# A two-convolution block on one core: one semaphore for each quarter of the parts, two kinds of transfers issued by ScalarE instead of SyncE, and the bias matmuls of a step in one block

## What is computed

```python
x = x + _L0_conv_ref(_gn(x), L0_conv_weight, L0_conv_scale)
x = x + _L1_conv_ref(_gn(x), ...)
# _L1_conv_ref: r = relu(bn(w_r x + b)); ker = w_s r + b_s
for ki in range(K):
    for kj in range(K):
        out = out + xp[:, :, :, ki:ki + H, kj:kj + W] * ker[:, :, ki * K + kj][:, :, None]
```

## Time and profile before

| | before |
|---|---|
| median of 3 runs | 2220.75 us (2215.48 to 2227.02) |
| profiled execution | 2222.71 us, span 2220.9 us |
| TensorE / VectorE / ScalarE / GpSimd busy | 78% / 61% / 48% / 46% |
| mean granted TensorE clock | 0.896 of full |
| DMA queues q1 (SyncE) and q10 (ScalarE), share of 16 engines | 77.3% and 3.5% |

### The profile page before, as it was taken

How to read it: one execution, slowest core, us unless ns; L and a number is a source line. 1 busy time by engine, 2 the same in 40 slices (tenths; PEclk the granted TensorE clock), 3 DMA queues, 4 the chain that set the end, 5 groups by cost and what they waited for, 6 DMA issues and landing times.

```text
span 2220.9 us, 39147 instructions
## 1 busy us (share of the span) xinstructions
PE 1724.5 (78%) x15168; PEld 737.5 (33%) x15168; DVE 1358.6 (61%) x1652; ACT 1061.5 (48%) x758; POOL 1020.8 (46%) x905
## 2 busy tenths in 40 slices
PE   3497878868798686877868788686986869878885
PEld 2242333323333232333323333232332323323332
DVE  5374756747477574765747567564764747657564
ACT  1354455535455453554534555454554535545453
POOL 2154444445355443554534444443553435544563
PEclk8798988989899897998989899898997989979897
DMA  4768888788888888888788798887888888887894
GB/s 96 181 179 198 205 200 217 194 194 206 195 206 220 196 201 190 204 210 204 203 197 198 191 214 210 193 215 181 205 217 189 191 191 207 208 195 196 198 250 117
DMA packets 224281, 436.46 MB, mean 197 GB/s; under 512 B 89214, under 2 KB 136751, under 8 KB 219951
## 3 DMA queue, kind: packets, MB, share of 16 engines
q1 hardware_dynamic: 207968, 408.27, 77.3%
q10 hardware_dynamic: 16128, 25.70, 3.5%
HBM read 336.06 MB, written 84.93 MB: 190 GB/s over the span
## 4 chain that ended last, share of the span: by engine, by line
issue 32%; POOL 29%; SPq 13%; DMA 10%; PE 7%; DVE 5%; ACT 3%; POOLq 0%; ACTq 0%; DVEq 0%
POOL folded L383 29%; DMA parts_dram<-parts 7%; SPq L318 6%; PE ybank L581 3%; SPq L288 3%; DVE prod L817 2%; SPq L258 2%; SPq L272 1%; DMA sums_dram<-osb 1%; DMA relu<-blocks 1%; PE ybank L523 1%; PE ybank L613 1%; ACT patches L449 1%; ACT blocks L459 1%; PE obank L592 1%
## 5 line engine op out<-in xcount | busy, mean ns | idle before, releaser
L383 POOL TENSOR_TENSOR folded<-prod 128x448 f32<-128x448 f32 x896 | 1009.1, 1140 | 1178.7 <-DVE prod L817 1178.5
L817 DVE TENSOR_TENSOR prod<-ybank,relu 128x896 f32<-128x896 f32 x896 | 960.8, 1090 | 379.9 <-PE ybank L581 312.7
L449 ACT ACTIVATE patches<-patches 64x1792 f16<-64x1792 f16 x448 | 745.4, 1708 | 514.0 <-DMA patches<-parts_dram 380.2
L581 PE MATMUL ybank<-patches,wspan 128*64 128x448 f16 x7168 | 863.6, 376 | 155.1 <-DVE prod L817 114.8
L581 PEld LDWEIGHTS ybank<-patches,wspan 128*64 128x64 f16 x7168 | 368.2, 114 | 674.3 <-issue 265.1
L592 PE MATMUL obank<-patches,wbias 128*32 128x448 f16 x3584 | 237.6, 390 | 118.5 <-ACT osb L437 118.5
L599 PE MATMUL obank<-folded,esum 128*32 128x448 f32 x1792 | 228.4, 583 | 1.5 <-POOL folded L383 1.5
L523 PE MATMUL ybank<-sgn,convw 128*128 128x448 bf16 x1008 | 205.1, 357 | 8.0 <-DVE prod L817 4.5
L613 PE MATMUL ybank<-back,blocks 128*128 128x128 f32 (+1 forms) x448 | 70.6, 310 | 168.7 <-ACT blocks L459 168.7
L829 DVE TENSOR_TENSOR xs<-ybank,xs 128x1024 f32<-128x1024 f32 (+1 forms) x64 | 61.9, 967 | 204.7 <-PE ybank L613 204.6
L592 PEld LDWEIGHTS obank<-patches,wbias 128*32 128x32 f16 x3584 | 79.2, 101 | 256.1 <-ACT osb L437 136.4
(11 more groups left out here) (92 smaller groups left out, 423.4 us busy)
## 6 DMA issues: line engine op xcount, KB each, us to landing
patches<-parts_dram SPq DMA_DIRECT2D x1232, 224.0 KB, 6.4
parts_dram<-parts SPq DMA_DIRECT2D x128, 256.0 KB, 2.8
xs<-x_dram SPq DMA_DIRECT2D x128, 196.0 KB, 5.0
sums_dram<-osb ACTq DMA_DIRECT2D x112, 224.0 KB, 5.7
rows<-sums_dram SPq DMA_DIRECT2D x112, 224.0 KB, 3.2
out_dram<-xs SPq DMA_DIRECT2D x128, 196.0 KB, 3.6
relu<-blocks SPq DMA_DIRECT2D x256, 49.0 KB
patches<-gb_dram SPq DMA_DIRECT2D x1, 784.0 KB
```

Source lines behind the costliest of these rows:

```text
L383: pool.tensor_tensor(folded[:, u % 8, :], prod[:, u % 2, 0, :], prod[:, u % 2, 1, :], ALU.add).then_inc(fold_done, 1)
L449: act.activation(X2[0:COPIED_ROWS, e % 2, at], X1[0:COPIED_ROWS, e % 3, at], ACT.Copy).then_inc(copied, 1)
L581: mm = pe.matmul(bank("unit", p, n)[64 * t:64 * t + 64, h, 0:N], wspan[0:STACK_ROWS[stack], stack, g, h, :], of_group(e, stack, g), start= ...
L817: dve.tensor_tensor(prod[:, u % 2].rearrange("m h (n c) -> m h n c", c=GC), bank("unit", p, n)[:, :, 0:N].rearrange("m h (n c) -> m h n c" ...
```

## The change

There are three edits.

1. `d_written` becomes four semaphores, one for each quarter. `parts_out(p, k)` now waits only until quarter k of the pair before has landed, `first_stack` waits for all four, and `high` for the quarter two before, whose buffer it writes again.
2. `rows` and `spread` are issued from ScalarE's queue. `spread(p + 1)` stands right after the second relu (unit 38), `spread(0)` before the first copies; `rows(e - 1)` stands at unit 7 of each step (`ROWS_AT`), behind the copies at units 4 and 5 and ahead of `sign` at unit 7 of the pair.
3. Both stacks of `bias(e)` are issued at unit 6 of the step; before, one was at unit 5 and one at unit 6.

```diff
--- before.py
+++ after.py
@@ -77,7 +77,7 @@
 RED_AT = {37: 0, 38: 1}
 OUT0_AT = {46: 0, 49: 1}
 ARRANGE1_AT, ARRANGE0_AT = 13, 43
-SUMS_B, BIAS, SUMS_A = 3, (5, 6), 7
+SUMS_B, BIAS, SUMS_A, ROWS_AT = 3, 6, 7, 7
 
 COPY_AT = {0: 0, 1: 1, 4: 2, 5: 3}
 
@@ -184,7 +184,7 @@
         t_ready = sem("t_ready")
         high_done = sem("high_done")
         low_done = sem("low_done")
-        d_written = sem("d_written")
+        d_written = [sem(f"d_written{k}") for k in range(4)]
         first_in = [sem("first_in0"), sem("first_in1"), sem("first_in2")]
         second_in = [sem("second_in0"), sem("second_in1")]
         copied = sem("copied")
@@ -266,11 +266,11 @@
             def parts_out(p, k):
 
                 sp.wait_ge(low_done, 4 * p + k + 1)
-                if 4 * p + k > 0:
-                    sp.wait_ge(d_written, DWRITE * (4 * p + k))
+                if p > 0:
+                    sp.wait_ge(d_written[k], DWRITE * p)
                 for l in range(2):
                     sp.dma_start(D[p % 2, l].rearrange("m (y h n) -> m y h n", y=2, h=4)[:, :, k, :],
-                                 Ev[:, l, k % 2]).then_inc(d_written, 16)
+                                 Ev[:, l, k % 2]).then_inc(d_written[k], 16)
 
             def plane(e, l, a):
 
@@ -283,7 +283,8 @@
                 if e >= 3:
                     sp.wait_ge(y_ready, GP * (e - 2))
                     sp.wait_ge(first_in[e % 3], FIRSTLOAD * (e // 3))
-                sp.wait_ge(d_written, DWRITE * 4 * (e // E + 1))
+                for k in range(4):
+                    sp.wait_ge(d_written[k], DWRITE * (e // E + 1))
                 for l, a, row, step in PLANES[0]:
                     sp.dma_start(X1[row:row + 15 * step + 1:step, e % 3, :],
                                  plane(e, l, a)).then_inc(first_in[e % 3], 16)
@@ -295,29 +296,6 @@
                 for l, a, row, step in PLANES[1][COPIED_PLANES:]:
                     sp.dma_start(X2[row:row + 15 * step + 1:step, e % 2, :],
                                  plane(e, l, a)).then_inc(second_in[e % 2], 16)
-
-            def rows(e):
-
-                p, eo = e // E, e % E % 4
-                group = 2 * p + (e % E) // 4
-                sp.wait_ge(sums_written, 16 * (e + 1))
-                if group > 0:
-                    sp.wait_ge(arranged, group)
-                if e > 0:
-                    sp.wait_ge(rows_in, 16 * e)
-                src = bass.AP(tensor=G.tensor, offset=(e % 2) * 128 * N, ap=[[JY * 8, 32], [8 * N, 16], [1, JY * 8]])
-                sp.dma_start(U[32 * eo:32 * eo + 32].rearrange("m g y n -> m g (y n)"), src).then_inc(rows_in, 16)
-
-            def spread(p):
-                sp.wait_ge(r_done, 2 * (p + 1))
-                if p >= 2:
-                    sp.wait_ge(prod_done, UNITS * (p - 1))
-                for t in range(2):
-                    for dy in range(PY):
-                        for h in range(HALVES):
-                            sp.dma_start(R[64 * t + 16 * dy:64 * t + 16 * dy + 16, p % 2, h, :],
-                                         rsum[32 * dy + OH * h:32 * dy + OH * h + OH].rearrange("o x n -> o (x n)")
-                                         ).then_inc(r_spread, 16)
 
             sp.dma_start(gmat[:], consts[:, C_G:C_E]).then_inc(first_loaded, 16)
             sp.dma_start(t_par, params).then_inc(first_loaded, 16)
@@ -339,7 +317,6 @@
             sp.wait_ge(zeroed, ZEROS)
             first_stack(0)
             second_stack(0)
-            spread(0)
             first_stack(1)
             for p in range(pairs):
                 for s in range(E):
@@ -348,8 +325,6 @@
                         second_stack(e + 1)
                     if e + 2 < EALL:
                         first_stack(e + 2)
-                    if e > 0:
-                        rows(e - 1)
                     if p + 1 < pairs:
                         if s == 3:
                             parts_out(p + 1, 0)
@@ -357,7 +332,6 @@
                         if s == 4:
                             parts_out(p + 1, 2)
                             parts_out(p + 1, 3)
-                            spread(p + 1)
                     if s == 2 and p > 0:
                         store(p - 1)
                     if s == 3 and p + 2 < pairs:
@@ -365,7 +339,6 @@
                             sp.wait_ge(stored, STORE * p)
                         sp.wait_ge(x_loaded, XLOAD * (p + 2))
                         load(p + 2)
-            rows(EALL - 1)
             store(pairs - 1)
             sp.wait_ge(stored, STORE * pairs)
 
@@ -417,7 +390,8 @@
             def high(p, k):
                 act.wait_ge(t_ready, 4 * p + k + 1)
                 if 4 * p + k >= 2:
-                    act.wait_ge(d_written, DWRITE * (4 * p + k - 1))
+                    before = 4 * p + k - 2
+                    act.wait_ge(d_written[before % 4], DWRITE * (before // 4 + 1))
                 act.activation(Ev[:, 0, k % 2], bank("t", p, k)[:], ACT.Copy).then_inc(high_done, 1)
 
             def relu(p, k):
@@ -430,6 +404,17 @@
                                bank("red", p, k)[:, :, 0:HW // POS],
                                ACT.Relu, bias=red_bias[:], scale=red_scale[:]).then_inc(r_done, 1)
 
+            def spread(p):
+                act.wait_ge(r_done, 2 * (p + 1))
+                if p >= 2:
+                    act.wait_ge(prod_done, UNITS * (p - 1))
+                for t in range(2):
+                    for dy in range(PY):
+                        for h in range(HALVES):
+                            act.dma_start(R[64 * t + 16 * dy:64 * t + 16 * dy + 16, p % 2, h, :],
+                                         rsum[32 * dy + OH * h:32 * dy + OH * h + OH].rearrange("o x n -> o (x n)")
+                                         ).then_inc(r_spread, 16)
+
             def gather(e):
                 act.wait_ge(osum_done, 2 * (e + 1))
                 if e > 0:
@@ -448,6 +433,18 @@
                 at = slice(COPY * j, COPY * (j + 1))
                 act.activation(X2[0:COPIED_ROWS, e % 2, at], X1[0:COPIED_ROWS, e % 3, at],
                                ACT.Copy).then_inc(copied, 1)
+
+            def rows(e):
+
+                p, eo = e // E, e % E % 4
+                group = 2 * p + (e % E) // 4
+                act.wait_ge(sums_written, 16 * (e + 1))
+                if group > 0:
+                    act.wait_ge(arranged, group)
+                if e > 0:
+                    act.wait_ge(rows_in, 16 * e)
+                src = bass.AP(tensor=G.tensor, offset=(e % 2) * 128 * N, ap=[[JY * 8, 32], [8 * N, 16], [1, JY * 8]])
+                act.dma_start(U[32 * eo:32 * eo + 32].rearrange("m g y n -> m g (y n)"), src).then_inc(rows_in, 16)
 
             def arrange(group):
 
@@ -468,6 +465,7 @@
             act.wait_ge(taps_ready, 1)
             for k in range(2):
                 relu(0, k)
+            spread(0)
             for j in range(JX):
                 copy_high(0, j)
 
@@ -479,10 +477,14 @@
                         high(p + 1, T_AT[n])
                     if more and n in RED_AT:
                         relu(p + 1, RED_AT[n])
+                    if more and n == max(RED_AT):
+                        spread(p + 1)
                     if n % GP == SUMS_B and e > 0:
                         gather(e - 1)
                     if n % GP in COPY_AT and e + 1 < EALL:
                         copy_high(e + 1, COPY_AT[n % GP])
+                    if n % GP == ROWS_AT and e > 0:
+                        rows(e - 1)
                     if more and n == STAT0_AT:
                         sign(p + 1)
                     if more and n == STAT2_AT:
@@ -493,6 +495,7 @@
                     if n == ARRANGE0_AT:
                         arrange(2 * p)
             gather(EALL - 1)
+            rows(EALL - 1)
             arrange(2 * pairs - 1)
 
         @block.tensor
@@ -639,8 +642,9 @@
                     e, i = E * p + n // GP, n % GP
                     if i == SUMS_B and e > 0:
                         sums(e - 1, 1)
-                    if i in BIAS:
-                        bias(e, BIAS.index(i))
+                    if i == BIAS:
+                        bias(e, 0)
+                        bias(e, 1)
                     if i == SUMS_A:
                         sums(e, 0)
                     if more and n == STAT0_AT:
```

## The result

| | before | after |
|---|---|---|
| median | 2221.97 us (4 runs) | 2136.72 us (2133.27 to 2144.95, 4 runs) |
| ratio | | 0.9623, 95% interval 0.9584 to 0.9662 |
| span of the profiled execution | 2220.9 us | 2132.4 us |
| mean granted TensorE clock | 0.896 | 0.898 |

The change saves 3.8%, 85 us. The forecast was 2069, 152 us; the range ended at 2135, so the time lies just outside it, beside what rival B gave (2134).

What follows compares the result with a forecast made beforehand. One chain was taken to bound each pair: relu, SyncE's queue, spread, landing, arrange, outputs. 129 + 8 + 20 - 5 = 152 us saved gave 2069 us; own range 2030 to 2105, full range 1970 to 2135.

Steps and rivals of the forecast that it cites:

- rival B: Late DMA landings at the spread's stage, or load-paced steps, halve the 129 us gain: 2134 us; chance 0.21.
- Rivals A and D: Spread's issue on ScalarE: A, cheap at 0.39 us apiece, 1967 us, chance 0.15; D, slow at 2.0 us, 2369 us, 0.04.
- The step that failed: At the spread's stage, step 3's rows land 3.2 us after issue, by 327 to some 329, for arrange.
- The share of 0.69: DMA engines' busy share from 310.94 to 335.67 us, the stretch behind the second relu.
- 17 us of work: DMA work of the stretch behind the relu (0.69 x 24.73), claimed to fit before 329.
- first term: Outputs at the spread's stage start 8.6 us sooner in each of 15 pairs: 129 us gained.
- All other terms together: Start +8, bias block and waits for osb +20, ScalarE's wait for the sums -5.
- A second term: Rows on ScalarE wait for the sums ahead of sign: loss of 0 to 2 us a pair, -5 in all.
- The start: Before the first steps, spread on ScalarE brings the first product 2.7 us sooner and removes a 4.88 us wait: +8.
- the +20 booked: Net gain in us from the bias block and earlier loads shortening TensorE's osb waits outside the spread's stage.
- Quarter semaphores by themselves: On SyncE, parts 2 and 3 cost some 2.5 us instead of 11.90; nothing counted beyond the other terms.
- rival C: At the spread's stage landings, not issue, set arrange, so moving the issue buys nothing: 2198 to 2221 us; chance 0.03.

Runs made afterwards that it cites:

- e1: The changed kernel with ScalarE issuing the rows of step 3 just ahead of spread instead of behind it; 2084 us.
- e6: The changed kernel with SyncE holding the 8 patches transfers for the next pair's step 0 until arrange is done; 2130 us.
- e2: The changed kernel with spread given back to SyncE, behind the parts of quarters 2 and 3; 2103 us.
- e9: The kernel before with quarter semaphores and the bias block; rows and spread stay on SyncE; 2060 us.
- e3: The changed kernel with rows given back to SyncE behind first_stack; spread stays on ScalarE; 2053 us.
- e4: The kernel before with the quarter semaphores alone; rows and spread on SyncE, bias in halves; 2078 us.
- e8: e3 with spread shared, 8 transfers issued by ScalarE and 8 by SyncE behind its parts; 2028 us.
- e10: e1 with the other rows issued five units later, when their sums have long been written; 2055 us.

## Why the prediction was wrong

**What held.** The queue on ScalarE went as written: spread's issue (11.6 us, forecast 12.0), copies, gather within half a microsecond, the bias block at the low clock (3.18, forecast 3.3), TensorE's longer wait for osb at this place (8.9, forecast about 8) and its near absence elsewhere. Rivals A and D, about the price of an issue on ScalarE, are out: the median is 689 ns against 682 on SyncE.

**The step that failed** is "`arrange` needs the rows issued at 323.4. They land 3.2 us later by the median, so 327, and up to some 329 on busy engines". They took 10.4 us. The 3.2 us were a median over all steps; the rows of this very step, the ones that `arrange` waits for, took 10.0 us before the change as well, and that could have been read from the same trace. Two more readings went with it. The share of 0.69 was a mean over 24.73 us; over the 16 us behind the relu it was 0.80 already. And the "17 us of work" left out the eleven patches transfers which, by the prediction's own words, would leave earlier into this stretch; with them it stands at 0.99. e1 and e6 show it from two sides: send the rows before the relu ends, or hold eight of the patches, and they are in time. Outputs lost 4.3 us by it in the pair shown and 5.0 in the mean (24.6 against 19.6), 75 us in 15 pairs, more than half of the first term: it gave some 50 us instead of 129. All other terms together gave some 35 instead of 23.

**A second term was mis-sized:** "I book a loss between 0 and 2 us a pair, 0.3 of it as the value: -5 in all" for ScalarE's wait for the sums. With spread on SyncE the move of `rows` costs 43 us (e2 against e9), and there the traces show this wait at work: outputs to conv grows by 4.1 us a pair. My loop of 10.3 against 12.06 us took the median landing of the sums, 5.7; in the step shown of e2 it is 8.3, and `sign` stands behind it. With spread on ScalarE, the changed kernel has only 1.2 us a pair more than e3 between outputs and conv, some 17 us. Of the 84 us between the two, 75 lie between relu and outputs, where the rows land late.

**What the other terms measured.** The start 4.8 instead of 8. TensorE's waits for osb outside this place fell from 43 us to 7, more than the +20 booked; but that the block itself brings it is shown only with everything on SyncE (18 us).

**And the credit was wrongly given.** "Quarter semaphores by themselves ... I count nothing beyond the above" left their worth inside the first term, under the title of the moved spread. e4 takes them alone: 144 us, close to my 152 for the whole. The rule of the Trainium skill that I made part of rival C (DMA: Bandwidth & Descriptors, Issuing engines are not separate DMA queues) said that another issuing engine saves issue time only. e3 against e9 agrees: 7 us, within the intervals. I had set the 11.90 us of waits against that rule, but those belong to the semaphore, not to the engine. Sharing the issue between both queues did pay: e8 is 25 us under e3.

In all, from the medians: quarters -144, bias block -18, spread to ScalarE -7, rows to ScalarE +84: 85 us, 2222 to 2137. The order matters, since the terms overlap.

**Rival B** gave the right time, 2134, and its first branch is what happened. I had it at 0.21 and ended the range 2 us short of the result. That its time fits so well is in part luck: "Half of 129 gone" was not worked out from a landing, the first term lost 75 us and not 65, and the other terms made up for it.

**Open.** Why outputs to conv is shorter with the bias in halves when the spread is on ScalarE; why the parts land later in e10 than in e1; and whether the spread's late landing in e8 (4.96 us) is the patches' doing, as in e1, which was not tried there.

## What to carry to other kernels

When a change has several edits that meet at one wait, price each of them alone against the same chain: here a shorter wait in the old queue was worth more than the whole, and the other two edits together took 59 us of it back. A transfer moved into a compute engine's queue brings its semaphore wait along, ahead of everything behind it; place it where that wait is already over (e10) or leave it on a queue that has nothing urgent behind. And price a landing by the rows of that very transfer at its place, not by the median of all its kind, with what else the change will send into the stretch.

## What the runs showed of the hardware

- A transfer of spread (16 partitions, 49 KB) takes 689 ns to issue on ScalarE (median of 256) and 682 on SyncE (256 in the kernel before); one of a 128-partition tile takes 326 ns on ScalarE. Sixteen of the first kind kept ScalarE from computing for 11.6 us.
- 224 KB of rows took 10.0 us to land before the change, issued from SyncE right behind eight 224 KB patches transfers, and 10.4 us after it, issued from ScalarE while eight others left from SyncE; with these held back (e6) they took 3.3.
